# A gated cross-attention block: unit loads, FFN inputs and FFN steps of the output stage in a new order

## What is computed

```python
def _L0_xattn_ref(hidden_states, key_value_states, attention_mask, position_bias, ln_weight, w_q, w_k, w_v, w_out):
    x = _rmsnorm(hidden_states, ln_weight)
    h_q, h_k, h_v = x @ w_q.T, key_value_states @ w_k.T, key_value_states @ w_v.T
    score = jnp.einsum('bqhd,bkhd->bhqk', h_q, h_k) + position_bias[None]
    score = softmax(where(m, score, -inf))
    attn = jnp.einsum('bhqk,bkhd->bqhd', score, h_v).reshape(b, lq, H * DH)
    return hidden_states + attn @ w_out.T
...
x = x + tanh(g_xattn[0]) * _L0_xattn_ref(_layernorm(x), ctx_4096, mask, ...)
x = x + tanh(g_ffn[0]) * _L0_ffn_ref(_layernorm(x), W_base, b_base, W_router, A, B)
```

## Time and profile before

| | us |
|---|---|
| median of 3 runs | 878.59 (877.77 to 879.08) |
| profiled execution | 878.36 |
| its span | 876.6 |
| PE busy | 837.9 (96% of the span) |
| DVE, ACT, POOL busy | 627.1, 494.6, 294.6 |
| mean granted clock of PE, share of full speed | 0.973 |
| DMA moved | 168.52 MB, 192 GB/s over the span |

### The profile page before, as it was taken

How to read it: one execution, slowest core, us unless ns; L and a number is a source line. 1 busy time by engine, 2 the same in 40 slices (tenths; PEclk the granted TensorE clock), 3 DMA queues, 4 the chain that set the end, 5 groups by cost and what they waited for, 6 DMA issues and landing times.

```text
span 876.6 us, 13049 instructions
## 1 busy us (share of the span) xinstructions
PE 837.9 (96%) x4318; PEld 708.8 (81%) x4318; DVE 627.1 (72%) x981; ACT 494.6 (56%) x1153; POOL 294.6 (34%) x310
## 2 busy tenths in 40 slices
PE   8899999999999999999999999999977799997888
PEld 7688887888888888888888888888865588875676
DVE  5776476577688888888788878887743687766345
ACT  4546655456666666666666666666643965542110
POOL 1213230013455563736536545555250000040120
PEclk9999999999999999999999999999998899998699
DMA  8365456595565466645556467557768988851001
GB/s 315 125 180 175 126 176 197 168 283 179 180 211 178 150 196 199 210 144 176 192 177 210 143 183 226 175 161 236 269 224 329 388 298 289 278 211 37 25 0 73
DMA packets 131298, 168.52 MB, mean 192 GB/s; under 512 B 9248, under 2 KB 83872, under 8 KB 130592
## 3 DMA queue, kind: packets, MB, share of 16 engines
q1 hardware_dynamic: 131232, 167.70, 59.2%
HBM read 111.04 MB, written 62.91 MB: 198 GB/s over the span
## 4 chain that ended last, share of the span: by engine, by line
PE 75%; DMA 7%; DVE 7%; ACT 3%; POOL 3%; issue 2%; SPq 2%; DVEq 0%; ACTq 0%; POOLq 0%
PE bank L324 60%; PE bank L1454 6%; PE bank L1471 5%; DMA t_raw<-t_spill 4%; PE bank L1462 3%; DVE t_hl L985 1%; DMA s_piece<-in_w_o 1%; ACT t_hl L861 1%; DMA t_spill<-g_at 1%; DMA raw_v<-in_w_v 1%; DVE stats L989 1%; DVE s_hl L985 1%; DVE wv L985 1%; DMA t_spill<-x_at 1%; DVE acc L1216 1%
## 5 line engine op out<-in xcount | busy, mean ns | idle before, releaser
L324 PE MATMUL bank<-t_hl,s_hl 128*128 128x512 f32 x672 | 172.9, 419 | 15.6 <-DVE s_hl L985 15.6
L324 PE MATMUL bank<-xb,wq 128*128 128x512 f32 x672 | 177.3, 399 | 0.0
L324 PE MATMUL bank<-cb,wq 128*128 128x512 f32 x672 | 177.2, 399 | 0.0
L324 PEld LDWEIGHTS bank<-t_hl,s_hl 128*128 128x128 f32 x672 | 135.6, 205 | 47.1 <-DVE s_hl L985 14.9
L324 PE MATMUL bank<-wv,cb 128*128 128x512 f32 x672 | 156.5, 394 | 4.2 <-DVE wv L985 3.8
L324 PEld LDWEIGHTS bank<-wv,cb 128*128 128x128 f32 x672 | 126.6, 189 | 32.9 <-DVE wv L985 5.9
L645 POOL TENSOR_TENSOR bm<-bias_sb,mneg 128x512 f32<-128x512 f32 x64 | 75.1, 1174 | 200.8 <-DVE pr L1146 165.0
L324 PEld LDWEIGHTS bank<-cb,wq 128*128 128x128 f32 x672 | 121.8, 188 | 23.0
L324 PEld LDWEIGHTS bank<-xb,wq 128*128 128x128 f32 x672 | 121.7, 188 | 22.9
L985 DVE TENSOR_TENSOR t_hl<-t_raw,t_hl 128x1024 fp32r<-128x1024 f32 x56 | 68.6, 1225 | 68.6 <-ACT t_hl L861 68.6
L861 ACT ACTIVATE t_hl<-t_raw 128x1024 fp32r<-128x1024 f32 x56 | 59.2, 1057 | 86.0 <-PE bank L324 54.2
(11 more groups left out here) (157 smaller groups left out, 1230.5 us busy)
## 6 DMA issues: line engine op xcount, KB each, us to landing
t_raw<-t_spill SPq DMA_DIRECT2D x56, 512.0 KB, 4.4
v_spill<-stage SPq DMA_DIRECT2D x64, 256.0 KB, 2.9
raw<-in_w_qk SPq DMA_DIRECT2D x32, 512.0 KB, 5.5
v_sb<-v_spill SPq DMA_DIRECT2D x64, 256.0 KB, 3.1
s_raw<-s_spill SPq DMA_DIRECT2D x56, 256.0 KB, 4.6
t_spill<-x_at SPq DMA_DIRECT2D x48, 256.0 KB, 3.3
s_piece<-in_w_o SPq DMA_DIRECT2D x64, 128.0 KB, 3.5
s_spill<-s_piece SPq DMA_DIRECT2D x32, 256.0 KB, 3.6
```

The lines of the kernel that those rows point to most:

```text
L324: mm = pe.matmul(dst, a, b, start=first and n == 0, stop=last and n == total - 1, skip_group_check=True)
```

## The change

1. `EARLY_LOADS` and `EARLY_SPLITS`: from the second step on, most units are loaded a step sooner; one split (unit 10) moves behind the steps. The loads behind the steps begin at unit 14.
2. SP's last `store_sums` go between the loads of units 14 to 16, and the waits for all stores go behind the load of unit 18.
3. x is loaded in eight pieces of 256 KB behind units 18, 20, 22, 24, 28, 30, 32 and 34, the bias behind 26, the router weights behind 36, the base weights in four pieces behind 38, 40, 42 and 44, the expert weights behind 46. ACT and DVE take each piece two units later.
4. The feed-forward's steps `center`, `tokens1_hi`, `tokens1_lo` and `finish` are per batch, and the orders on ACT, DVE and PE are written anew. The first output transposes stand one unit sooner.
5. In the value stage the third token sum goes from POOL to DVE.

```diff
 EARLY_SPLITS = {(PAIRS - 2, 1): (0,), (PAIRS - 2, 2): (1,), (PAIRS - 2, 3): (2, 3), (PAIRS - 1, 0): (4,), (PAIRS - 1, 1): (5, 6),
-                (PAIRS - 1, 2): (7, 8), (PAIRS - 1, 3): (9, 10)}
-EARLY_LOADS = {(PAIRS - 2, 0): (0, 1), (PAIRS - 2, 1): (2, 3), (PAIRS - 2, 2): (4,), (PAIRS - 2, 3): (5,), (PAIRS - 1, 0): (6, 7),
-               (PAIRS - 1, 1): (8,), (PAIRS - 1, 2): (9, 10), (PAIRS - 1, 3): (11, 12)}
-FIRST_SPLIT = 11
-FIRST_LOAD = 13
-
-
-
-ACT_X1 = (48, 50, 53, 54, 55)
-DVE_X1 = (44, 45, 48, 50, 51, 53, 54, 55)
+                (PAIRS - 1, 2): (7, 8), (PAIRS - 1, 3): (9,)}
+EARLY_LOADS = {(PAIRS - 2, 0): (0, 1), (PAIRS - 2, 1): (2, 3, 4), (PAIRS - 2, 2): (5,), (PAIRS - 2, 3): (6,), (PAIRS - 1, 0): (7, 8),
+               (PAIRS - 1, 1): (9, 10), (PAIRS - 1, 2): (11, 12), (PAIRS - 1, 3): (13,)}
+FIRST_SPLIT = 10
+FIRST_LOAD = 14
+
+X2_AT = (18, 20, 22, 24, 28, 30, 32, 34)
+BB_AT = 26
+LORA_AT = 36
+BASE_AT = (38, 40, 42, 44)
+UP_AT = 46
...
-            for s in range(STEPS, STEPS + 3):
-                store_sums(s)
-            for h in range(2):
-                sp.wait_ge(x_stored[h], 16 * 3 * DUOS)
-                sp.wait_ge(y_stored[h], 16 * DUOS)
-            sp.wait_ge(z_stored, 16 * 2 * DUOS)
-            sp.wait_ge(g_stored[0], 16 * 3 * DUOS)
-            sp.wait_ge(g_stored[1], 16 * DUOS)
             for n in range(FIRST_LOAD, UNITS):
                 load_o(n)
-                if n == FIRST_LOAD + 1:
-                    for own, at in ((slice(0, HALF), HALF), (slice(HALF, B), 0)):
-                        sp.dma_start(acc[:, own, :], x[:, at:at + HALF, :]).then_inc(x2_in, 16)
-                if n == FIRST_LOAD + 4:
-                    sp.dma_start(raw_base[:, :, :].rearrange("p c n -> p (c n)"), w_base).then_inc(base_in, 16)
-                if n == FIRST_LOAD + 6:
+                if n < FIRST_LOAD + 3:
+                    store_sums(STEPS + n - FIRST_LOAD)
+                if n == X2_AT[0]:
+
+                    for h in range(2):
+                        sp.wait_ge(x_stored[h], 16 * 3 * DUOS)
+                        sp.wait_ge(y_stored[h], 16 * DUOS)
+                    sp.wait_ge(z_stored, 16 * 2 * DUOS)
+                    sp.wait_ge(g_stored[0], 16 * 3 * DUOS)
+                    sp.wait_ge(g_stored[1], 16 * DUOS)
+                if n in X2_AT:
+                    t = X2_AT.index(n)
+                    sp.dma_start(acc[:, t, :], x[:, ORDER[t], :]).then_inc(x2_in[t], 16)
+                if n == BB_AT:
+                    sp.dma_start(bb[:, :], b_base).then_inc(bb_in, 16)
+                if n == LORA_AT:
                     sp.dma_start(raw_lora[:, :, :].rearrange("p c n -> p (c n)"), w_lora).then_inc(lora_in, 16)
+                if n in BASE_AT:
+                    c = BASE_AT.index(n)
+                    sp.dma_start(raw_base[:, c, :], w_base[:, D * c:D * c + D]).then_inc(base_in[c], 16)
+                if n == UP_AT:
                     sp.dma_start(raw_up[:, :], w_up).then_inc(up_in, 16)
-                    sp.dma_start(bb[:, :], b_base).then_inc(bb_in, 16)
...
             pool.wait_ge(ctx_in[1, 1], 16)
-            pool.wait_ge(wv_lo_ok, 3)
+            pool.wait_ge(wv_lo_ok, VORD.index(M5) + 1)
             token_sum(2, ctx_q, ct_ok, cb_lo_ok)
-            token_sum(3, ctx_q, ct_ok, cb_lo_ok)
             pool.wait_ge(ctx_in[1, 0], 16)
+            pool.wait_ge(ct_ok, 3)
+            pool.wait_ge(wv_lo_ok, VORD.index(M7) + 1)
             token_sum(4, ctx_q, ct_ok, cb_lo_ok)
...
-            act.wait_ge(gs_ok, 1)
-            for n in range(FIRST_SPLIT, UNITS):
-                o_hi(n)
-                if n == DUOS + 3:
-                    o_copy(0)
-                if n == FIRST_SPLIT + 4:
-                    act.wait_ge(x2_in, 32)
-                    for t in range(B):
-                        act.activation(acc[:, t, :], acc[:, t, :], ACT.Identity, bias=gated[:, 1, ORDER[t]:ORDER[t] + 1],
-                                       scale=gated[:, 0, ORDER[t]:ORDER[t] + 1]).then_inc(acc_ok, 1)
-                if n in (2 * DUOS + 3, 3 * DUOS + 3):
-                    o_copy(n // DUOS - 1)
-                if n == FIRST_SPLIT + 10:
-                    act.wait_ge(base_in, 16)
-                    act.activation(base_hi[:, :, :], raw_base[:, :, :], ACT.Copy).then_inc(ffn_hi_ok, 1)
-                if n == FIRST_SPLIT + 12:
+            def ffn_hi(n):
+
+                if n - 2 in X2_AT:
+                    t = X2_AT.index(n - 2)
+                    act.wait_ge(x2_in[t], 16)
+                    act.activation(acc[:, t, :], acc[:, t, :], ACT.Identity, bias=gated[:, 1, ORDER[t]:ORDER[t] + 1],
+                                   scale=gated[:, 0, ORDER[t]:ORDER[t] + 1]).then_inc(acc_ok, 1)
+                if n - 2 == LORA_AT:
                     act.wait_ge(lora_in, 16)
                     act.activation(lora_hi[:, :, :], raw_lora[:, :, :], ACT.Copy).then_inc(ffn_hi_ok, 1)
+                if n - 2 in BASE_AT:
+                    c = BASE_AT.index(n - 2)
+                    act.wait_ge(base_in[c], 16)
+                    act.activation(base_hi[:, c, :], raw_base[:, c, :], ACT.Copy).then_inc(ffn_hi_ok, 1)
+                if n - 2 == UP_AT:
                     act.wait_ge(up_in, 16)
                     act.activation(up_hi[:, :], raw_up[:, :], ACT.Copy).then_inc(ffn_hi_ok, 1)
-                if n == ACT_X1[0]:
-                    tokens1_hi(0)
-                if n == ACT_X1[1]:
-                    router_exp(0)
-                if n == ACT_X1[2]:
-                    hwt_hi(0)
-                if n == ACT_X1[3]:
-                    tokens1_hi(1)
-                if n == ACT_X1[4]:
-                    router_exp(1)
-
+
+            act.wait_ge(gs_ok, 1)
+            for n in range(FIRST_SPLIT, 51):
+                o_hi(n)
+                ffn_hi(n)
+                if n in (DUOS + 3, 2 * DUOS + 3, 3 * DUOS + 3):
+                    o_copy(n // DUOS - 1)
+            tokens1_hi(0)
+            o_hi(51)
+            tokens1_hi(1)
+            o_hi(52)
+            o_hi(53)
+            o_hi(54)
+            tokens1_hi(2)
+            o_hi(55)
+            tokens1_hi(3)
+            router_exp(0)
+            hwt_hi(0)
+            o_copy(NP - 1)
+            router_exp(1)
             hwt_hi(1)
-            o_copy(NP - 1)
-            tokens1_hi(2)
+            tokens1_hi(4)
+            tokens1_hi(5)
             router_exp(2)
-            tokens1_hi(3)
+            tokens1_hi(6)
+            tokens1_hi(7)
             hwt_hi(2)
...
+                    if i == 2:
+                        ve.wait_ge(ctx_in[1, 1], 16)
+                        ve.wait_ge(ct_ok, 2)
+                        ve.wait_ge(cb_lo_ok, VORD.index(M5) + 1)
+                        ve.tensor_tensor(tt[0], ctx_q(1, 1), ctx_q(0, 1), ALU.subtract).then_inc(ct_ok, 1)
...
+            def ffn_lo(n):
+                if n - 2 == BB_AT:
                     ve.wait_ge(bb_in, 16)
                     ve.tensor_scalar(bb[:, :], bb[:, :], tg[:, 1:2], None, ALU.mult).then_inc(bg_ok, 1)
-                if n == 4 * DUOS + 3:
+                if n - 2 == LORA_AT:
+                    ve.wait_ge(ffn_hi_ok, 1)
+                    lo(lora_lo[:, :, :], raw_lora[:, :, :], lora_hi[:, :, :]).then_inc(ffn_lo_ok, 1)
+                if n - 2 in BASE_AT:
+                    c = BASE_AT.index(n - 2)
+                    ve.wait_ge(ffn_hi_ok, c + 2)
+                    lo(base_lo[:, c, :], raw_base[:, c, :], base_hi[:, c, :]).then_inc(ffn_lo_ok, 1)
+                if n - 2 == UP_AT:
+                    ve.wait_ge(ffn_hi_ok, DC + 2)
+                    lo(up_lo[:, :], raw_up[:, :], up_hi[:, :]).then_inc(ffn_lo_ok, 1)
+
+            ve.wait_ge(consts_ok, E + 1)
+            for n in range(FIRST_SPLIT, 45):
+                o_lo(n)
+                ffn_lo(n)
+                if n == 4 * DUOS + 2:
                     o_sum(3)
-                if n == 5 * DUOS + 3:
+                if n == 5 * DUOS + 2:
                     o_sum(4)
-                if n == DVE_X1[0]:
-                    add_output(0)
-                if n == DVE_X1[1]:
-                    add_output(1)
-                    center(0)
-                if n == DVE_X1[2]:
-                    tokens1_lo(0)
-                if n == DVE_X1[3]:
-                    routing(0)
-                if n == DVE_X1[4]:
-                    o_sum(5)
-                if n == DVE_X1[5]:
-                    hwt_lo(0)
-                    add_output(2)
-                if n == DVE_X1[6]:
-                    add_output(3)
-                    center(1)
-                    finish(0)
-                if n == DVE_X1[7]:
-                    tokens1_lo(1)
+            add_output(0)
+            add_output(1)
+            o_lo(45)
+            o_lo(46)
+            ffn_lo(46)
+            add_output(2)
+            o_lo(47)
+            o_lo(48)
+            ffn_lo(48)
+            center(0)
+            o_lo(49)
+            center(1)
+            o_lo(50)
```

(88 more changed lines are left out.)

62 lines of the change are left out of this document (24 added, 38 removed).

## The result

The changed kernel takes 825.12 us (median of 4 runs, 823.86 to 826.02) against 878.18 for the kernel before beside it (876.86 to 879.08): ratio 0.9396, 95% interval 0.9378 to 0.9414. The profiled execution took 826.02 us with a span of 824.1, so 1.9 lie outside the span, as before.

The account below looks back on a forecast made before the run. PE was taken as the bound between two stretches of waits, each wait also slowing the clock. Gains of 21.0 + 23.5 + 3.2 = 47.7 us from 878.36 gave 830.7 us; range 824.5 to 844.

Parts of the forecast that it names:

- the sum of all upper ends: Whole kernel: upper gains of the parts, 23.6 + 26.1 + 3.4 = 53.1 us, giving 825.3 us.
- part A: Attention to output stage: loads a step sooner, stores and store waits moved back, gain 21.0 us (ends 10 and 23.6).
- part B: Output stage: x, base and router weights loaded in pieces, 15 transfers instead of 6; cost 0, at worst 1 to 2 us.
- The unit's pitch: Output units on PE: 312 matmuls fill 72.6 us, 0.232 each, so a unit of twelve takes 2.79 us.
- the 22.6 of losses: Output stage on PE: 19.9 us lost from unit 8 to unit 16, plus 2.7 at unit 7.
- Part C: Tail: feed-forward steps per batch and new orders give handovers units of cover, gain 23.5 us (ends 9 and 26.1).
- Part D: Value stage: one token sum from POOL to DVE removes PE's 2.24 us wait and slow clock, 3.2 (ends 0.5 and 3.4).
- the allowance of 1.6 us: Output stage: taken off the loads' gain because DMA of units 11 and 12 has no slack before PE wants unit 11.
- Rival 1: Tail: center(2) waits for POOL's rstd1(1) behind add_bias; two or three handovers missed, 840 to 845 us, chance 0.17.
- Rivals 2 and 3: 2: loads don't get ahead, 842 us, chance 0.13. 3: new tail order does little, 845 us, chance 0.04.
- rival 2's second half: Attention to output stage: ACT's copy still stands behind a landing load, gain only 10, 842 us; rival's chance 0.13.
- Rival 4: Last attention steps: SP's sooner loads wait for splits, holding the value load; at 8 us a step 887, chance 0.02.

Follow-up runs that it names:

- e11: Changed kernel with load tables, store waits, whole loads and whole FFN passes as before; only new tail order and token sum kept: 847.49 us, ratio 0.9644.
- e2: Changed kernel with the early load and split tables as before; stores and store waits stay moved: 837.35 us, ratio 0.9513.
- e3: Changed kernel with SP's last sums and all store waits back ahead of unit 14's load: 830.10 us, ratio 0.9429.
- e7: Changed kernel with x in two 1 MB transfers, base weights in one, x's eight ACT passes as a block, FFN splits whole: 831.83 us, ratio 0.9465.
- e6: Changed kernel with the tail orders of ACT, DVE and PE as before, output transposes one unit later: 850.94 us, ratio 0.9689.
- e1: Changed kernel with the third token sum back on POOL: 829.23 us, ratio 0.9425.
- e4: Changed kernel with unit 11 loaded a step sooner and unit 10 split ahead of ACT's last attention copy: 825.19 us, ratio 0.9383.
- e9: Changed kernel with unit 11 loaded a step sooner and units 10 and 11 both split ahead of ACT's last attention copy: 824.52 us, ratio 0.9372.

## Why the prediction came out as it did

The forecast was 830.7 us, the result 825.1: faster, inside the range, 5.6 us below the forecast and 0.2 below the sum of all upper ends. Its mechanism held, in that the waits it named went and PE became the bound. But the parts were sized wrongly, and that the sum came so near is in part luck: part A was set some 4 us or more too high and part B, set at nothing, gave 6.5, which nearly cancel.

**Part A, 21.0 forecast.** A and B together gave 23.2 by the markers, and 22.2 to 22.7 in e11. Of this e2 gives 10.3 to 12.2 to the tables, e3 2.9 to 6.1 to the store waits, e7 6.3 to 6.8 to the pieces. So part A as the prediction defined it is worth 13 to 17 (A and B less e7: 15 to 17), and 21.0 was too high for it. The step that failed is the one that booked the whole loss of 42.2 - 22.3 us between unit 8 and unit 16 under the loads and stores. A part of that hole belonged to the 1 MB loads of x and to the eight passes on them, and the trace of before shows it on ACT:

```profile
679.34 1.06 ACT L861 ACTIVATE t_hl<-t_raw 128x1024 fp32r<-128x1024 f32 x1 [5.35 <-DMA t_raw<-t_spill]
...
680.82 5.74 ACT L950 ACTIVATE acc<-acc,gated 128x512 f32<-128x512 f32 x8
686.46 1.04 ACT L861 ACTIVATE t_hl<-t_raw 128x1024 fp32r<-128x1024 f32 x1
```

Unit 15's load, issued at 668.08 behind the two of x, comes after 11.3 us, and PE waits 3.16 us before unit 15. Unit 16's split stands behind the block, and PE waits the 2.58 us at 689.51 for it. (The prediction puts the block before unit 15; it stands between the splits of 15 and 16.) With the tables mended the same two things open a hole further on, before units 19 and 21 of e7.

**Part B, 0 forecast.** It is worth 6.3 to 6.8 (e7). The prediction weighed only whether pieces cost more than whole loads; it noted that the eight passes would no longer stand ahead of a split, but gave that no price. It even wrote that x and base went "into the hole at 667 to 690", and did not ask what they would do once the hole was closed. Its estimate of the load, 343 GB/s needed where 340 were there, was low on both sides for a while: measured are 393 GB/s at a share of 1.03 from 660 to 700, then 341 at 0.97 from 700 to 732, with PE never idle. The cost was 0, and the gain was left out.

**The unit's pitch, 2.79 us.** It is 2.73. The group of 312 matmuls from which it was taken begins behind a wait of 2.58 us, and in the window 690 to 692 of the trace of before the clock is 0.50. The 26 units take 761.94 - 689.51 = 72.43 us where 26 x 2.73 = 71.0 are due: about 1.4 us of slow clock were averaged into the pitch. With 2.73 the 22.6 of losses are some 24.5: 759.2 - 647.29 - 33 x 2.73 = 21.8 from unit 8 to 40, and the 2.7 at unit 7.

**Part C, 23.5 forecast, ends 9 and 26.1.** 25.2 by the markers, 25.9 to 26.6 in e6. The floor for PE was right: 87.3 us from the end of unit 40 to the last steps of DVE were worked out, and 820.09 - 731.89 = 88.2 measured. The term that was mis-sized is the 2.6 us taken off for one half-missed handover and a slow clock after a lora: the only wait of PE in the tail is 0.19 us, and the clock is 1.00 from 760 to 820. x1_transposes(0), called the tightest, was not waited for at all, nor was any hw_transposes. Which of the new orders does the work was not tried apart.

**Part D, 3.2 forecast, end 3.4.** 4.15 by the markers, 4.0 in e1, above its upper end. The size of the clock's share failed: "33.4 are due" for 144 matmuls used the pitch 0.232. In the changed kernel 168 of them start in 38.0 us (167 steps of 0.2276), so 144 are due in 32.9 and some 1.6 were lost, not 1.1. "No wait at 31 us" held.

**The named signs.** Loads of 9 and 10: 634 to 636 expected, 630.1 and 631.2 measured. Unit 16: 663 to 668 expected, 663.7. PE over 98% busy from 640 on: just missed, 97.7%; clock 1.00 as named. "No wait over 1 us between unit 8 and 55": missed, 2.57 at unit 10. That is the sign named for a fault of part A between units 9 and 14, and the allowance of 1.6 us for it was of the right order. But the cause given, the DMA of units 11 and 12, is not the one: it is ACT's copy behind POOL's sum, shown by the chain, by e4 and by e9. Following ACT's order by hand I had let POOL's sums out, which the copy needs.

**Rival 1, a wait in the tail behind POOL.** Its place was right and its price nil, but by a hair. DVE waits for rstd1(1) 0.61 us, center(2) then ends at 762.40, and x1_transposes(2) starts at 762.45. The tokens of x1_transposes(3) are as close (765.69 and 765.75). The prediction's "under 2 us to spare" was in truth 0.05 or so, and that neither became a wait was luck. Two operations of add_bias took 2.81 and 2.21 us, 5.0 together, not 9.65. DVE and POOL in the tail of the changed kernel:

```profile
761.85 0.55 DVE L1242 TENSOR_SCALAR xn<-acc,mv,scales 128x512 f32<-128x512 f32 x1 [0.61 <-POOL scales L711]
```

```profile
749.06 2.81 POOL L716 TENSOR_TENSOR acc<-acc,bb 128x512 f32<-128x512 f32 x1 [7.96 <-DVE xn L1242]
752.24 2.21 POOL L716 TENSOR_TENSOR acc<-acc,bb 128x512 f32<-128x512 f32 x1 [0.37 <-DVE xn L1242]
```

Both still ran beside DVE's splits and took longer than the 1.28 of the shortest of their kind. **Rivals 2 and 3** would have left 10 of part A or 9 of part C; neither did. Something near rival 2's second half is what costs the one wait of 1.7 to 2.6 us: the copy stands behind a late sum of POOL, not behind a landing load, and once, not in each step. **Rival 4**, SP held in each step, shows nowhere: at the scores of the last step PE is ahead by 4.15 us, which is what part D is worth.

## What to carry to other kernels

When a hole in an engine's work is to be closed, list everything that was done in the hole: what used it for free needs a place of its own afterwards, and here that was worth 6.5 of 23 us. That goes for the passes of an engine as much as for the loads: the longer wait of e7 stood behind eight passes of ACT. Take the pitch of the bounding engine from a stretch whose windows all show the full clock, not from a group that begins behind a wait. And when one engine's order is followed, follow too who must release the buffer of each copy in it: the one wait that was left hung on a sum of the least loaded engine. Last, ask how close each handover came, and not only whether it waited: two of this tail's had 0.05 us to spare.
